# Eight own and three shared slots in two alternating bank pairs, with later own chunks added to the standing product

## The reference

```python
h = jnp.maximum(_layernorm(x, axis=-1), 0.0)
# layer 0, W1 is (128, 192), W2 is (192, 64)
mask = (adj > 0.0)
xj_proj = x @ W1a
diff = x[:, :, None, :] - x[:, None, :, :]
h = relu(xj_proj[:, :, None, :] + diff @ W1b + b1)
hm = einsum('bjkh,bjk->bjh', h, mask)
deg = sum(mask, axis=-1)
out = hm @ W2 + deg[..., None] * b2
```

## Time and profile before

| | us |
|---|---|
| median of three runs | 1898.67 |
| the profiled execution | 1900.7 |
| its span, first to last instruction | 1899.0 |
| layer 0, from the first own one-hot to the last update | 53 to 1373 |
| TensorE busy in the span | 1679.3 (88%) |
| VectorE busy | 1344.1 (71%) |
| ScalarE busy | 974.1 (51%) |
| GpSimd busy | 600.4 (32%) |

### The profile page before, as it was taken

One profiled execution on the slowest core, in us unless ns is written; L12 is line 12 of the kernel. 1 busy time (PEld: TensorE's weight loads), 2 busy tenths in 40 slices (PEclk: granted clock), 3 DMA queues, 4 the chain that ended last, 5 costly groups with the idle time before them and its releaser, 6 DMA issues. The chain is left out here.

```text
span 1899.0 us, 49116 instructions
## 1 busy us (share of the span) xinstructions
PE 1679.3 (88%) x13581; PEld 1277.4 (67%) x13582; DVE 1344.1 (71%) x3728; ACT 974.1 (51%) x2265; POOL 600.4 (32%) x706
## 2 busy tenths in 40 slices
PE   1899999999999899999999999899899998994399
PEld 0676666666667676666767666677688897960276
DVE  5688887877888778788877878788734444457633
ACT  2555554545554555554545555454155554745555
POOL 0343433434434444434433334344300000026300
PEclk9999999999999999999999999999989998997699
DMA  5000000000000000000000000000000000000011
GB/s 120 7 12 7 7 6 6 6 6 12 6 6 6 6 8 10 6 6 6 6 6 8 10 6 6 6 0 1 1 0 0 0 0 1 0 0 0 11 40 39
DMA packets 40222, 18.57 MB, mean 10 GB/s; under 512 B 18792, under 2 KB 40106, under 8 KB 40106
## 3 DMA queue, kind: packets, MB, share of 16 engines
q1 hardware_dynamic: 39574, 17.28, 3.8%
q10 hardware_dynamic: 532, 0.21, 0.1%
HBM read 13.29 MB, written 4.19 MB: 9 GB/s over the span
## 5 line engine op out<-in xcount | busy, mean ns | idle before, releaser
L532 PE MATMUL bank<-ac_lo,work 128*128 128x192 f16 x2495 | 528.6, 246 | 0.0
L532 PE MATMUL bank<-ac_hi,work 128*128 128x192 f16 x2495 | 528.6, 246 | 0.0
L781 POOL TENSOR_TENSOR acc<-acc 128x384 f32<-128x384 f32 x256 | 267.2, 1065 | 734.3 <-DVE acc L738 734.3
L726 DVE SCALAR_TENSOR_TENSOR acc<-bank,acc 128x384 f32<-128x384 f32 (+1 forms) x1060 | 466.0, 494 | 12.5 <-PE bank L532 6.6
L524 PE MATMUL bank<-ac_hi,ident 128*128 128x384 f16 (+1 forms) x1060 | 326.7, 308 | 89.6 <-DVE acc L726 48.0
L702 DVE TENSOR_SCALAR work<-work,slot_key 128x896 f16 (+2 forms) x393 | 271.7, 691 | 90.5 <-issue 88.3
L524 PE MATMUL bank<-ac_lo,ident 128*128 128x384 f16 (+1 forms) x1060 | 324.4, 306 | 0.0
L532 PEld LDWEIGHTS bank<-ac_lo,work 128*128 x2495 | 244.0, 98 | 68.3 <-issue 0.2
L532 PEld LDWEIGHTS bank<-ac_hi,work 128*128 x2495 | 243.8, 98 | 68.4 <-issue 0.2
L637 ACT ACTIVATE hmTa<-bank,unscale 128x128 f32<-128x128 f32 x128 | 47.1, 368 | 444.9 <-PE bank L496 444.9
L524 PEld LDWEIGHTS bank<-ac_hi,ident 128*128 128x128 f16 x1060 | 103.3, 97 | 174.4 <-DVE acc L735 91.2
(11 more groups left out here) (204 smaller groups left out, 3129.4 us busy)
## 6 DMA issues: line engine op xcount, KB each, us to landing
adj_in<-in_adj_dram SPq DMA_DIRECT2D x32, 256.0 KB, 2.9
out_dram<-acc SPq DMA_DIRECT2D x32, 128.0 KB, 2.0
l1w<-in_L_gnn_W_dram SPq DMA_DIRECT2D x2, 64.0 KB
l1b<-in_L_gnn_b_dram SPq DMA_DIRECT2D x2, 64.0 KB
x_all<-in_x_dram SPq DMA_DIRECT2D x4, 0.2 KB, 11.7
nm_in<-in_nodemask_dram ACTq DMA_DIRECT2D x1, 64.0 KB
w1a<-in_L_gnn_W_dram ACTq DMA_DIRECT2D x1, 48.0 KB
w1b<-in_L_gnn_W_dram ACTq DMA_DIRECT2D x1, 48.0 KB
```

Source lines behind the costliest of these rows:

```text
L532: last = nc.tensor.matmul(ps[:, t * H:(t + 1) * H], hot, part[:, q, H:2 * H], start=False, stop=(e == 1 and t == slots - 1))
L726: nc.vector.scalar_tensor_tensor(out=sums, in0=bank[n_bank][:, 0:slots * H], scalar=0.0, in1=sums, op0=ALU.min, op1=ALU.add).then_inc(s_fr ...
L781: last = nc.gpsimd.tensor_tensor(t[:, 0:2 * H], t[:, 0:2 * H], t[:, 2 * H:4 * H], ALU.add)
```

## The change

Own chunks have 8 slots, the shared chunk 3. The slots lie 256 numbers apart, two in a bank, and one tensor spans four banks: two *pairs* of two banks, four slots in each. An own chunk is two halves of four slots, one in each pair, and each half is one sum of 768 numbers on VectorE (`dve_half`) in the place of two sums of 384 (or of 384 and 192). The shared chunk is one read of 576 numbers. With 8 and 3 slots every one of the 128 graphs has two own chunks in these inputs, none a third.

Only the first own chunk is seeded. For the later one VectorE subtracts the old one-hot from the new (`dve_difference`, the values are -1, 0 and 1), and TensorE adds difference times C to what stands in PSUM, A + C_old, which gives A + C_new. So the later half needs no seed, but it needs the difference, and the same pair must have been summed.

In VectorE's step `between()` is split. `dve_update` (of the graph three back, it was two) comes between the two own chunks' sums (`halfway`). The preparation of the next group comes after the read of the shared chunk (`after`). The outer loop carries a hint about its branch on VectorE only. The accumulator of the shared chunk is doubled, and `pool_sum` adds 192 numbers of it in the place of 384.

```diff
-    OWN = [(0, 0, 0, 2), (1, 1, 2, 2), (2, 5, 4, 2), (3, 6, 6, 1)]
-    SHARED = [(0, 0, 0, 2), (1, 1, 2, 2), (3, 6, 4, 1)]
-    SC = 7
-    SS = 5
+    SU = 4
+    SC = 2 * SU
+    SS = 3
+    SB = 2
+    SW = 256
...
+        def unit(pair, first, count):
+
+            return slots[:, pair * SU * SW:(pair + 1) * SU * SW].rearrange("p (t c) -> p t c", c=SW)[:, first:first + count, 0:H]
...
         def pe_slots(pe, b, g, u, q, regs, between):
...
-            with pe.Fori(0, n - 1):
-                pe_chunk(pe, q, OWN, ident16[:, :], regs)
-                pe.reg_add(regs[2], regs[2], 1)
+            at = next_chunk()
+            if not (known(b) and b == 0):
+                pe.wait_ge(s_free[1], prev)
+            pe_half(pe, 0, q, at, cnt)
+            if not (known(b) and b == 0):
+                pe.wait_ge(s_free2, b)
+            pe_half(pe, 1, q, at, cnt)
+            with pe.Fori(0, n):
+                at = next_chunk()
+                pe.reg_add(later, later, 1)
+                pe.wait_ge(s_D, later)
+                pe.wait_ge(s_free[0], prev)
+                pe_next_half(0, q, at)
+                pe.wait_ge(s_free[1], prev)
+                pe_next_half(1, q, at)
             between()
             pe.wait_ge(s_host, g + 1)
-            pe_chunk(pe, q, SHARED, host[:, u, q * N:(q + 1) * N], regs)
+            pe.wait_ge(s_free[0], cnt)
+            pe_seeds(q % 2, SS, host[:, u, q * N:(q + 1) * N], q)
+            pe.wait_ge(s_G2, b + 1)
+            pe_gathers(q % 2, SS, lambda t: onehot2[:, t * N:(t + 1) * N], q).then_inc(s_done2, 1)
...
-            with eng.Fori(1, NI - 1) as i:
+            with nc.Fori(1, NI - 1, engines=bass.OrderedEngineSet([eng.engine]),
+                         hint_back_edge=prefetch_back_edge) as i:
...
+        def dve_difference(dve, pos, old):
+
+            at, at_old = (dve.snap(r, min_val=0, max_val=CH) for r in (pos, old))
+            nc.vector.tensor_tensor(onediff[:, ds(at, CH)], onehot[:, ds(at, CH)], onehot[:, ds(at_old, CH)],
+                                    ALU.subtract).then_inc(s_D, 1)
...
+        def dve_slots(dve, b, g, u, q, regs, halfway, after):
...
+            with dve.Fori(0, n) as c:
+                dve.reg_mov(old, pos)
+                dve_onehot(dve, rs[:, u, q, :, :], c + 1, pos)
                 dve.reg_mov(prev, cnt)
                 dve.reg_add(cnt, cnt, 1)
+                dve.wait_ge(s_G, cnt)
+                dve_difference(dve, pos, old)
+                dve.wait_ge(s_done[0], prev)
+                dve_half(0, q)
+                dve.wait_ge(s_done[1], prev)
+                dve.wait_ge(s_free[0], prev)
+                dve_half(1, q)
+            halfway()
+            dve.wait_ge(s_done[0], cnt)
+            dve.wait_ge(s_free[1], prev)
+            dve_half(0, q)
+            dve_shared_onehot(dve, g, u, q)
+            dve.wait_ge(s_done[1], cnt)
+            dve.wait_ge(s_free[0], cnt)
+            dve_half(1, q)
...
+            dve.wait_ge(s_done2, b + 1)
+            nc.vector.tensor_scalar(acc2[:, q % 2, :].rearrange("p (t h) -> p t h", t=SS), unit(q % 2, 0, SS),
+                                    0.0, None, ALU.min).then_inc(s_free2, 1)
+            after()
```

More of the change, by code:

```diff
@@ L506, in pe_update, with pe_seeds @@
             nc.tensor.matmul(pU, hmTb[:, p, q * N:(q + 1) * N], w2b[:, :], start=False, stop=True).then_inc(s_W2, 1)
[L508 to L522, removed]
+        def pe_seeds(pair, count, node, q):
+            for t in range(0, count, SB):
+                n = min(SB, count - t)
@@ L529, in pe_chunk, with pe_gathers @@
[L529 to L534, removed]
-        def pe_slots(pe, b, g, u, q, regs, between):
+        def pe_gathers(pair, count, hot, q, seeded=True):
+            for t in range(count):
+                for e, part in enumerate((ac_hi, ac_lo)):
+                    last = nc.tensor.matmul(unit(pair, t, 1), hot(t), part[:, q, H:2 * H].unsqueeze(1),
+                                            start=False, stop=(e == 1 and (t % SB == SB - 1 or t == count - 1)),
+                                            skip_group_check=not seeded)
+            return last
@@ L697, in dve_first_rows @@
             dve.wait_ge(s_nop, 12 * g + 12)
-            nc.vector.tensor_tensor(host[:, p, :], host[:, p, :], past[:, :], ALU.subtract).then_inc(s_host, 1)
-        def dve_onehot(ranks, slots, key, at):
-            nc.vector.tensor_scalar(onehot[:, ds(at, slots * N)], ranks.rearrange("p t j -> p (t j)"),
-                                    slot_key[:, ds(key, 1)], None, ALU.is_equal).then_inc(s_G, 1)
-        def dve_slots(dve, b, g, u, q, regs, between):
-            cnt, prev, full, full_prev, pos, count_reg = regs
-            n = dve.snap(count_reg, min_val=MINC + 1, max_val=MAXC)
-            def count():
+            nc.vector.tensor_tensor(host[:, p, :], host[:, p, :], past, ALU.subtract).then_inc(s_host, 1)
@@ L796, in _ @@
             def _(pe):
-                regs = [pe.alloc_register(f"pe_{r}") for r in ("chunk", "chunk_before", "own_before", "ring_place")]
+                regs = [pe.alloc_register(f"pe_{r}")
+                        for r in ("own_chunk", "own_chunk_before", "onehot_place", "difference")]
                 pe.reg_mov(regs[0], 0)
                 pe.reg_mov(regs[2], 0)
+                pe.reg_mov(regs[3], 0)
                 pe_adj(pe, 0, 0, 0)
@@ L850, in _ @@
                 act_ac(act, 1, 1)
[L851 removed]
+                act_pads(act, 0, 0, 0, 0)
                 act_rank_nodes(act, 0)
@@ L881, in _ @@
                 regs = [dve.alloc_register(f"dve_{r}")
-                        for r in ("chunk", "chunk_before", "own", "own_before", "ring_place", "slot_chunks")]
+                        for r in ("own_chunk", "own_chunk_before", "onehot_place", "onehot_place_before", "later_chunks")]
                 dve.reg_mov(regs[0], 0)
@@ L888, in _, with halfway, after @@
                 dve.wait_ge(s_rs, 1)
-                dve_onehot(rs[:, 0, 0, :, :], SC, 0, 0)
-                dve.wait_ge(s_acc0, 1)
+                dve_onehot(dve, rs[:, 0, 0, :, :], 0, regs[2])
                 dve.wait_ge(s_n, 1)
-                dve.reg_load(regs[5], chunks[0:1, 0:1])
+                dve.reg_load(regs[4], chunks[0:1, 0:1])
                 def step(b, g, u, q, nxt, p, use):
-                    def between():
+                    def halfway():
+                        if not (known(b) and b < 3):
+                            dve_update(dve, b - 3)
+                    def after():
                         if nxt is not None:
@@ L902, in between @@
                                 dve_first_rows(dve, nxt, p)
-                        if not (known(b) and b < 2):
-                            dve_update(dve, b - 2)
-                    dve_slots(dve, b, g, u, q, regs, between)
-                all_iterations(dve, step)
-                for b in range(B - 2, B):
+                    dve_slots(dve, b, g, u, q, regs, halfway, after)
+                all_iterations(dve, step, prefetch_back_edge=True)
+                for b in range(B - 3, B):
                     dve_update(dve, b)
```

155 lines of the change are left out of this document (74 added, 81 removed).

## The result

The changed kernel takes 2209.39 us (median of four runs, 2206.68 to 2215.39), the kernel before in the same comparison 1898.50. The ratio is 1.1642, 95% interval 1.1617 to 1.1667: 311 us slower, where 115 were forecast, and outside the range. The profiled execution has a span of 2204.3 us; its mean granted clock is 0.872, that of before 0.974.

The account below looks back on a forecast made before the run. Neither TensorE nor VectorE is full; the chain of waits through both sets the step: 7.4 + 1.3 + 0.6 = 9.3, plus 1.8 for GpSimd, 11.1 against 10.2 us, x 128 = 115 us slower, 2014 us; range 1830 to 2090.

Parts of the forecast that it names:

- GpSimd's stops: VectorE's operations behind the shared read wait for GpSimd's instructions: 1.8 us a step on average, ends 0 and 3.7.
- TensorE's clock falls: Rival, chance 0.08: after waits of some 4 us TensorE runs at half clock, some 290 us on top, 2300.
- half of that if it recovers quickly: Within the falling-clock rival: half of its some 290 us on top, if TensorE's clock recovers quickly.
- The chain of 9.3 us: Linked waits between shared reads: 7.4 us, plus 1.3 VectorE preparation and 0.6 TensorE preparation a step, before GpSimd's stops.
- TensorE's own work that comes early hides beside VectorE's part: In each step's chain: A and C and the next graph's first chunk add no time.
- 7.4 + 0.74: Chain of one step without VectorE preparation, 7.4 us, plus 0.74 of TensorE's preparation in `between()`.
- the prediction's links: Chain pieces after the first sum: second sum 0.95, hand-back and gathers 0.71, transposes and update 1.39, shared chunk 1.26 us.
- Difference 0.68 us: VectorE's subtraction of 1024 float16 numbers for the later own chunk: 0.68 us, ends 0.42 and 0.84.
- Sums of 951 ns: VectorE's sum of 768 numbers for half an own chunk: 951 ns, four of them 3.8 us.
- Only wide operations block: Rival, chance 0.17: small operations of rows and counts pass GpSimd, waits 1.1 on average, step 10.4, +26 us: 1925.
- The hint: At VectorE's loop back edge: should remove the 3.94 us gap, costing 2.2 us a round, 31 us in all.
- TensorE's saving comes through: Rival, chance 0.25: little waits for GpSimd; step 9.3 with waits of 0, 1784 us, or 9.8 with 0.5, 1848.

Follow-up runs that it names:

- GpSimd later: Against the changed kernel, GpSimd starts a step's sums only once VectorE has made the next step's one-hot difference: 1909.67 us, ratio 1.0063 to the kernel before.
- wait filled: Against the changed kernel, TensorE makes the second seeded half three times over in three of four steps, two for nothing: 2097.70 us, ratio 1.1046.

## Why the prediction was wrong

The sign was right, and so was the chain of waits that ends at the difference. The size was not: 115 us forecast, 311 measured. Step by step:

| per step, us | predicted | measured | from |
|---|---|---|---|
| chain with preparation, GpSimd out of the way | 9.3 | 10.28 | GpSimd later |
| GpSimd's stops | 1.8 | 1.27 | wait filled, less that |
| clock | 0 | 1.10 | changed kernel, less wait filled |
| sum | 11.1 | 12.65 | changed kernel |

The measured terms are differences of stretches of four steps and add up by construction. Whole runs give 10.29 for the first kernel and 11.76 for the second, so 1.47 for the stops with what clock was still missing there, and 0.88 for the clock.

- **"TensorE's clock falls ... Chance 0.08"** is the step that failed: the forecast put the clock at nothing. Its own text had the waits (4 us in the steps with preparation) and the row of what follows one. It even announced 3 us of idle time a step as a sign that it was right, and then took the clock at 1.00. Its "half of that if it recovers quickly" was 145 us; filling the waits gave back 112, and 1.10 x 128 = 141 is an estimate from the stretch at full clock. It belonged into the sum, and 115 + 145 = 260 would have been the forecast.
- **The chain of 9.3 us** is the second: 0.98 us a step short, 125 us over the layer. GpSimd's stops were forecast 0.53 too high, 68 us, which hid half of it, and that is luck. Most of the 0.98 lies in two places, the next two points.
- **"TensorE's own work that comes early hides beside VectorE's part"** fails in the step without preparation. There TensorE has, behind the shared gathers, the next group's adjacency to transpose, A and C, and the first half, and VectorE waits 1.32 us for that half even with GpSimd out of the way: 10.02 us where the prediction's sum without stops gives 7.4 + 0.74 = 8.1. That is 1.9 in one step of four, half of the 0.98 (0.6 of the 1.9 belong to the next point). GpSimd's stops are free in that step (3.35 us from the shared read to the first sum, with them and without), which is part of why they cost less than 1.8.
- **From the first sum to the next shared read** every step is 0.4 to 0.6 us longer than the prediction's links. Part of that is the step from the last difference gather to the transposes, 0.38 us from start to start in the rows below and 0.25 to 0.39 in other steps, where the kernel before has 0.08 (636.11 to 636.19). What makes it longer is not shown. GpSimd later:

```profile
839.96 0.25 PE L532 MATMUL slot_banks<-ac_lo,onediff 128*128 128x192 f16 x1
840.34 0.32 PE L504 MATMUL bank<-ident,hm 128*128 128x128 f32 x1
```

The step without preparation, GpSimd later:

```profile
844.54 0.76 DVE L798 TENSOR_SCALAR work<-slot_banks 128x576 f32<-128x576 f32 x1 [2.09 <-PE slot_banks L532]
845.22 0.48 DVE L742 TENSOR_SCALAR work<-work,slot_key 128x1024 f16 x1
845.88 0.69 DVE L754 TENSOR_TENSOR onediff<-work  x1 [0.19 <-DVE work L742]
847.89 0.96 DVE L760 SCALAR_TENSOR_TENSOR acc<-slot_banks,acc 128x768 f32<-128x768 f32 x1 [1.32 <-PE slot_banks L532]
```

- **Stops by step.** From the shared read to the first sum the changed kernel took 6.78 us (first rows), 5.17 (rows) and 5.69 (counts); the prediction's terms give 2.08 + 2.10 + 1.7 = 5.88, 5.30 and 6.34. With GpSimd later it is 4.31, 3.45 and 4.29, so the stops are 2.47, 1.72 and 1.40, with nothing in the fourth step 1.40 on average. The first rows were undersized because each of eight comparisons can be stopped, not one; the counts oversized.
- **Difference 0.68 us**: 0.69 alone, 1.13 to 1.21 beside GpSimd. Sums of 951 ns: 953. These terms held.
- **"Only wide operations block"** falls: four numbers were stopped to 770 ns. The rule of the Trainium skill (SBUF — State Buffer, Who interferes with whom) that the prediction weighed agrees here: by it the four-number operations with two SBUF inputs wait, and `left` (L709) took 0.45 us at 844.12. One with a single SBUF input and scalars (L720, 0.77) was stopped as well; whether it falls under the rule's two-port modes this trace does not tell.
- **The hint** was forecast to remove 31 us of stall. In the kernel before, the hint is worth 12.5 us, and the changed kernel does not have the gap, with the hint or without.
- **"TensorE's saving comes through" at 1784** was the best case of this chain. Two kernels with the preparation out of it reached 1784 and 1786; that the number agrees is chance, since the rival kept the preparation in the chain. The best, 1777, gave the saving up again.

## What to carry to other kernels

Ask of every operation that moves whether the slower of two engines that hand work to each other now waits for it: 2.1 us of preparation in one step of four cost 5.2 us there, and the whole of it 405 us against a place three lines earlier, where VectorE waited for TensorE anyway. When a forecast says that TensorE will stand in every step for about as long as in a row behind which the granted clock fell, put the clock into the sum, priced from that row, and not among the rivals. Work saved on TensorE by making it depend on one more result of a slower engine is worth only what the dependence leaves: here seeding anew was faster in both orders tried.

## What was not expected of the hardware

- Useless products made the kernel 112 us faster (2209 to 2098), through the clock; at a full clock they cost 169.
- In the stretches read, waits of TensorE of 3.2 to 3.9 us in layer 0 came with a lower clock behind them, waits up to 2.4 with 1.00. The length of the wait did not settle it: with the later chunk seeded again and the preparation in place, full pace followed a wait of 2.71 us that ended at 608.48, and half pace a wait of 2.71 us that ended at 655.67.
- VectorE operations on 4 numbers a partition (float32 or int32) took 0.44 to 0.77 us beside GpSimd's sums, 0.17 without. A row of four comparisons took 2.11 in the place of 0.74. The sums that read PSUM did not stretch: 953 ns in the changed kernel, 949 with GpSimd later.
- VectorE's gap of 3.94 us at a loop round vanished with a change of code alone.
